# Reordering the softmax, transpose and bookkeeping steps of a causal-attention loop, and the layer-norm and transpose steps of the gating stage, in an eight-core transformer layer

## The chip, the cores and the metric

The kernel runs as one program on the 8 cores of one Trainium2 chip. Each core works on its own share of the rows and no core waits for another. The metric is device time in microseconds (us) of the slowest core. Each core has TensorE (PE: matmuls and transposes, reading SBUF and writing PSUM), VectorE (DVE), ScalarE (ACT), GpSimd (POOL) and SyncE (SP), which run side by side; each works through its own queue in the order of the program, and queues wait for one another on semaphores.

## The reference, cut to what matters

```python
# x: (2, 8192, 1024) float32
def attn(z, qk, ov):                     # one head, width 1024
    scores = einsum('bsd,de,bte->bst', z, qk, z) / 32
    scores = where(causal, scores, -inf)
    return einsum('bst,btd,de->bse', softmax(scores), z, ov)

def ffn(z):                              # 16 experts of width 512, 4 chosen, and a shared one
    scores = softmax(z @ gate_w.T)       # best 2 of 4 groups, then best 4 experts
    y = sum_e c[:, e] * ((silu(z @ w1[e]) * (z @ w3[e])) @ w2[e])
    return y + (silu(z @ ws1) * (z @ ws3)) @ ws2

x = x + attn(layernorm(x)); x = x + ffn(layernorm(x))
```

## The kernel before

Four cores share one of the two sequences. A core owns 16 query tiles (slots m = 0 to 15) of 128 rows, every fourth tile of its sequence; the first stage projects its own rows to Q and the second does the attention, the third the second layer norm with the gating, the fourth the experts. The sums of all slots stay in SBUF in `ACC`.

**Attention.** Keys and values are the normalised rows of the whole sequence. They are made on every core in 8 panels of 1024 rows, each of 8 tiles, into double buffers: V (`VP`) row-wise, K (`KP`) transposed. Panel p is used by slots 2p to 15, so panel 0 has 16 steps, panel 1 has 14, and panel 7 has 2. While panel p is used, panel p+1 is produced in between (`emit_prod_load`, `emit_prod_tp`):

- A load (L394, three buffers `STG`) and a layer norm (`ln_chain`): two passes over the tile on DVE (L254 and L258, sum and sum of squares), three tiny DVE operations (L262 to L268), then on ACT three tiny ones (L271 to L277) and the normalising pass (L281).
- Eight transposes on PE into the single PSUM buffer `PSPT2B` (L403), and one copy into `KP`: on DVE for even tiles (L410), on ACT for odd ones (L414).

A step i of the loop `do_panel`, which treats slot m, puts into the queues, in this order:

- `emit_qk`: 16 matmuls for the scores into `PS_SE` or `PS_SO`, alternating (L437; the first slot has 8, and the first two slots add a mask, L428).
- `emit_softmax`: DVE takes the negated row maximum (L452) and updates the running one (L456, or L460 to L466); ACT takes the exponential of the change (alpha, L469, from panel 1 on), then that of the scores into `PBF` with the row sum (L472); DVE updates the running sum (L478 or L482), which waits for that row sum.
- `emit_t` for step i-1: 8 transposes of `PBF` on PE (L491) into the single PSUM buffer `PSPT` and an ACT copy to `PTS` (L497). The transposes wait for exp(i-1) and for the copy of step i-2.
- `emit_pv` for step i-2: 16 matmuls into the single `PS_PV` (L508), then DVE rescales and adds to `ACC` (L517, or L520).
- Layer norms of the next panel, spread evenly over the steps (two at a time in panels 5 and 6), and transposes of tiles that are four behind.

After the last step come the two outstanding transposes and products, the remaining four production transposes, and `emit_finalize` for two slots: reciprocal (L530), scaling (L534), transposes (L539), the product with `ov` (L556) and the residual (L564, L571).

**Gating.** For each of 16 slots: `do_tt_ln(m)` (layer norm of `ACC` as above, then on DVE a cast to bf16, L716, and the remainder, L719), `do_tt_tp(m)` (PE transposes L726 and ACT copy L732 of the cast; PE transposes L737 and ACT copy L743 of the remainder), and `do_tt_gate(m)` (24 small matmuls L760 on both copies, then the DVE copy L769). The loop is staggered by hand: at m it emits gate(m-2), transposes(m-1), layer norm(m). A chain of small DVE operations then picks the experts, and the experts follow.

Of the kernel before, what the change touches and what calls it, by code (L numbers as in the profile page):

```python
# [166 lines left out]
def build_program(attn_only=False):  # L167
# [21 lines left out]
    with contextlib.ExitStack() as stk:  # L189
# [101 lines left out]
        with (  # L291
# [69 lines left out]
            with (  # L361
# [83 lines left out]
                    P.group("tensor", fns, reads=rd, writes=[rSP], inc="pe")  # L445
                    return nkt, SP, rSP

                def emit_softmax(p, i, m, nkt, SP, rSP):
                    par = i % 2
                    al = i % 3  # L450
                    ext = nkt * 128
                    P.emit("vector", lambda v: v.reduce_max(  # L452
                        smc(C_NRM + par), SP[:, 0:ext], axis=AX.X, negate=True),
                        reads=[rSP], writes=[rNRM[par]], inc="ve")
                    if p == 0:
                        P.emit("vector", lambda v: v.tensor_copy(  # L456
                            smc(C_NM + m), smc(C_NRM + par)),
                            reads=[rNRM[par]], writes=[rNM[m]], inc="ve")
                    else:
                        P.emit("vector", lambda v: v.tensor_sub(  # L460
                            smc(C_TMD + par), smc(C_NRM + par), smc(C_NM + m)),
                            reads=[rNRM[par], rNM[m]], writes=[rTMD[par]])
                        P.emit("vector", lambda v: v.tensor_scalar_min(
                            smc(C_TMD + par), smc(C_TMD + par), 0.0),
                            reads=[rTMD[par]], writes=[rTMD[par]])
                        P.emit("vector", lambda v: v.tensor_add(  # L466
                            smc(C_NM + m), smc(C_NM + m), smc(C_TMD + par)),
                            reads=[rTMD[par], rNM[m]], writes=[rNM[m]], inc="ve")
                        P.emit("scalar", lambda s: s.activation(  # L469
                            smc(C_ALPHA + al), smc(C_TMD + par), AF.Exp),  # L470
                            reads=[rTMD[par]], writes=[rALPHA[al]], inc="sc")
                    P.emit("scalar", lambda s: s.activation(  # L472
                        PBF[:, par * 1024: par * 1024 + ext], SP[:, 0:ext], AF.Exp,
                        bias=smc(C_NM + m), accum_out=smc(C_RSUM + par)),
                        reads=[rSP, rNM[m]], writes=[rPBF[par], rRSUM[par]],
                        inc="sc")
                    if p == 0:
                        P.emit("vector", lambda v: v.tensor_copy(  # L478
                            smc(C_LL + m), smc(C_RSUM + par)),
                            reads=[rRSUM[par]], writes=[rLL[m]], inc="ve")  # L480
                    else:
                        P.emit("vector", lambda v: v.scalar_tensor_tensor(  # L482
                            smc(C_LL + m), smc(C_LL + m), smc(C_ALPHA + al),
                            smc(C_RSUM + par), ALU.mult, ALU.add),
                            reads=[rRSUM[par], rALPHA[al]], writes=[rLL[m]],
                            inc="ve")
# [94 lines left out]
                def do_panel(p):  # L581
                    buf = p % 2
# [4 lines left out]
                    hist = []  # L587
                    for i, m in enumerate(slots):
                        nkt, SP, rSP = emit_qk(p, buf, i, m)
                        emit_softmax(p, i, m, nkt, SP, rSP)  # L590
                        hist.append((p, buf, i, m, nkt))
                        if i >= 1:
                            emit_t(*hist[i - 1])
                        if i >= 2:
                            emit_pv(*hist[i - 2])
                        want_ld = (len(prod) * (i + 1) + n - 1) // n
                        while nld < min(want_ld, len(prod)):
                            emit_prod_load(*prod[nld])
                            nld += 1
                        while ntp < nld - 4:  # L600
                            emit_prod_tp(*prod[ntp])
                            ntp += 1
                    emit_t(*hist[-1])
                    if len(hist) >= 2:
                        emit_pv(*hist[-2])
                    emit_pv(*hist[-1])
                    while nld < len(prod):
                        emit_prod_load(*prod[nld])
                        nld += 1
# [5 lines left out]
                for p in range(NPANEL):  # L615
                    do_panel(p)
# [36 lines left out]
        if True:  # L653
# [43 lines left out]
            if True:  # L697
# [75 lines left out]
                for m in range(NSLOT):  # L773
                    if m >= 2:
                        do_tt_gate(m - 2)
                    if m >= 1:
                        do_tt_tp(m - 1)
                    do_tt_ln(m)
                do_tt_tp(NSLOT - 1)
                do_tt_gate(NSLOT - 2)  # L780
                do_tt_gate(NSLOT - 1)
# [180 lines left out]
def _get_nc(attn_only=False):  # L962
    if attn_only not in _CACHED:
        _CACHED[attn_only] = build_program(attn_only)
    return _CACHED[attn_only]
# [50 lines left out]
```

How the kernel before makes its waits and increments, by code:

```python
        def body(engobj, e):  # L110
            for fn, waits, inc, inc_by in qs[e]:
                for s, v in waits:
                    engobj.wait_ge(self.semh[s], v)
                inst = fn(engobj)
                if inc is not None:
                    inst.then_inc(self.semh[inc], inc_by)
```

## Time and profile before

| | us |
|---|---|
| median of 2 runs | 2742.2 (2741.36 to 2743.04) |
| the profiled execution, time | 2740.59 |
| its span, slowest core (core 6) | 2738.7 |
| spans of the 8 cores | 2729.5 to 2738.7 |
| granted TensorE clock, mean of each core | 0.932 to 0.934 of full speed |
| attention, core 6 | about 206 to 1047 |
| gating, core 6 | about 1047 to 1200 |
| experts, core 6 | about 1200 to the end |

Over the span PE is busy 2287.7 us (84%), DVE 1120.8 (41%) and ACT 638.3 (23%). The page's share of busy time mixes the stages: the experts take more than half of the span with PE nearly always busy, and neither the attention nor the gating looks like them. The time outside the span is 2740.59 - 2738.7 = 1.9 us.

### The profile page before, as it was taken

The page shows a single profiled execution, that of the slowest core. Times are in us where ns is not written, and L with a number is a line of the kernel's source. Part 1 is how long each engine was busy: PE and PEld are TensorE (multiplying, and loading weights), DVE is VectorE, ACT ScalarE, POOL GpSimd, SP SyncE. Part 2 cuts the span into 40 slices and gives each one's busy share as a digit, 9 for nine tenths or more (in the row PEclk, how much of TensorE's full clock was granted, in tenths as well). Part 3 has the DMA queues.
Part 4 walks back from the last instruction along what each step waited for, and adds up shares of the span by engine and source line. Part 5 has one row for each costly group of instructions (what it writes and reads, how often), then busy time and mean ns, then how long its engine had stood idle before and what let it go on. Part 6 is the DMA issues. An engine that isn't in the chain of part 4 may idle for free.

```text
span 2738.7 us, 34373 instructions; the slowest of 8 cores (2729.5 to 2738.7 us)
## 1 busy us (share of the span) xinstructions
PE 2287.7 (84%) x11568; PEld 1058.0 (39%) x11568; DVE 1120.8 (41%) x1647; ACT 638.3 (23%) x949; POOL 32.9 (1%) x66
## 2 busy tenths in 40 slices
PE   1649898978676563359999999999999999999998
PEld 0324444434333232234444444444444444444443
DVE  3335454546456434533323443233432343422433
ACT  3544434434344323520011000110001100011000
POOL 0000000000000000000000000000000000000000
PEclk9969999999998786579999999999999999999999
DMA  6121010201102202022120221202212022120203
GB/s 141 46 80 37 16 62 16 74 35 47 48 31 77 74 19 55 1 47 46 31 47 16 47 47 31 47 16 47 47 31 46 16 47 47 33 45 16 47 0 123
DMA packets 28373, 121.97 MB, mean 45 GB/s; under 512 B 2864, under 2 KB 7216, under 8 KB 21552
## 3 DMA queue, kind: packets, MB, share of 16 engines
q0 software_dynamic: 11936, 60.98, 12.0%
q1 hardware_dynamic: 16272, 58.79, 6.4%
q8 instruction: 103, 1.69, 0.3%
q14 instruction: 62, 0.51, 0.1%
HBM read 172.36 MB, written 8.39 MB: 66 GB/s over the span
## 4 chain that ended last, share of the span: by engine, by line
PE 55%; DVE 1%; issue 0%; DVEq 0%
PE H L886 36%; PE H L912 18%; DVE APR L900 1%; DVE ACC L923 0%; DVEq L113 0%; DVE ACC L929 0%
## 5 line engine op out<-in xcount | busy, mean ns | idle before, releaser
L886 PE MATMUL H<-XF,W1B 128*128 128x512 bf16 x2304 | 522.9, 380 | 14.8 <-PEq L118 14.3
L912 PE MATMUL H<-W2B,APR 128*128 128x512 bf16 x2304 | 505.5, 378 | 29.4 <-DVE APR L900 29.0
L886 PE MATMUL H<-XF,W3B 128*128 128x512 bf16 x2304 | 520.8, 379 | 0.0
L900 DVE TENSOR_TENSOR APR<-SCRF,H 128x1024 bf16<-128x1024 f32 x144 | 175.9, 1221 | 824.5 <-PE H L886 824.5
L896 ACT ACTIVATE SCRF<-H 128x1024 f32<-128x1024 f32 x144 | 147.5, 1024 | 1346.8 <-PE H L886 1346.7
L923 DVE SCALAR_TENSOR_TENSOR ACC<-H,CC,ACC 128x1024 f32<-128x1024 f32 x256 | 328.7, 1284 | 147.4 <-PE H L912 147.0
L886 PEld LDWEIGHTS H<-XF,W1B 128*128 128x128 bf16 x2304 | 224.7, 98 | 290.2 <-issue 23.8
L912 PEld LDWEIGHTS H<-W2B,APR 128*128 128x128 bf16 x2304 | 206.8, 97 | 328.1 <-issue 118.5
L886 PEld LDWEIGHTS H<-XF,W3B 128*128 128x128 bf16 x2304 | 225.4, 98 | 271.8
L508 PE MATMUL PS_PV<-VP,PTS 128*128 128x512 bf16 x1088 | 266.5, 401 | 17.8 <-DVE ACC L520 11.5
L508 PEld LDWEIGHTS PS_PV<-VP,PTS 128*128 128x128 bf16 x1088 | 107.8, 102 | 149.8 <-issue 49.1
L254 DVE TENSOR_SCALAR_CACHE_REDUCE XLNBF<-STG 128x1024 bf16<-128x1024 f32 x80 | 97.3, 1216 | 116.3 <-DMA STG<-x_seq 70.8
L403 PE MATMUL PSPT2B<-IDB,VP 128*128 128x128 bf16 x512 | 47.6, 248 | 105.2 <-ACT SM L274 26.8
L437 PE MATMUL PS_SO<-KP,Q 128*128 128x512 bf16 x576 | 133.8, 386 | 0.0
L437 PE MATMUL PS_SE<-KP,Q 128*128 128x512 bf16 x512 | 120.0, 387 | 0.0
L258 DVE SCALAR_TENSOR_TENSOR XLNBF<-STG 128x1024 bf16<-128x1024 f32 x80 | 98.0, 1226 | 8.6
L520 DVE SCALAR_TENSOR_TENSOR ACC<-ACC,SM,PS_PV 128x1024 f32<-128x1024 f32 x56 | 71.7, 1280 | 68.5 <-PE PS_PV L508 67.1
L491 PE MATMUL PSPT<-IDB,PBF 128*128 128x128 bf16 x544 | 45.7, 230 | 53.9 <-ACT PTS L497 53.7
L322 PE MATMUL PSPT<-IDB,XLNBF 128*128 128x128 bf16 x128 | 16.2, 306 | 85.3 <-ACT XLNT L328 45.7
L271 ACT ACTIVATE SM<-SM,CONST 128x1 f32<-128x1 f32 x96 | 28.2, 294 | 253.4 <-DVE SM L268 253.1
L403 PEld LDWEIGHTS PSPT2B<-IDB,VP 128*128 128x128 bf16 x512 | 38.3, 111 | 119.6 <-issue 113.0
L437 PEld LDWEIGHTS PS_SO<-KP,Q 128*128 128x128 bf16 x576 | 56.8, 100 | 66.9 <-issue 5.8
(117 smaller groups left out, 1297.1 us busy)
## 6 DMA issues: line engine op xcount, KB each, us to landing
STG<-x_seq SPq DMA_DIRECT2D x64, 512.0 KB, 3.6
W1B<-w_img POOLq DMA_DIRECT2D x16, 1024.0 KB, 7.9
W3B<-w_img POOLq DMA_DIRECT2D x16, 1024.0 KB, 9.3
W2B<-w_img POOLq DMA_DIRECT2D x16, 1024.0 KB, 7.8
STG<-x_own SPq DMA_DIRECT2D x16, 512.0 KB, 4.0
XOWNF<-x_own SPq DMA_DIRECT2D x16, 512.0 KB, 4.5
out<-ACC SPq DMA_DIRECT2D x16, 512.0 KB, 2.7
OVB<-ov_img POOLq DMA_DIRECT2D x1, 2048.0 KB, 22.3
```

The source lines that it names most:

```text
L254: P.emit(se, lambda v: v.tensor_scalar(dump, src_ap, 1.0, 0.0, ALU.mult, ALU.add, accum_out=c(LN_MSUM)), reads=[src_res], writes=[rl, rdump])
L258: P.emit(se, lambda v: v.scalar_tensor_tensor(dump, src_ap, 1.0, src_ap, ALU.mult, ALU.mult, accum_out=c(LN_SSQ)), reads=[src_res], writes ...
L403: fns = [(lambda t, dch=dch: t.transpose(PSPT2B[:, dch * 128:(dch + 1) * 128], vslice(buf, kt, dch * 128, 128), IDB[:, :])) for dch in ran ...
L437: sp_=sp_: t.matmul(SP[:, bank * 512:(bank + 1) * 512], qsl(dch, m * 128, 128), kslice(buf, dch, bank * 512, 512), start=st, stop=sp_))
L491: fns = [(lambda t, kt=kt: t.transpose(PSPT2[:, kt * 128:(kt + 1) * 128], PBF[:, par * 1024 + kt * 128: par * 1024 + (kt + 1) * 128], IDB[ ...
L508: fns.append(lambda t, kt=kt, half=half: t.matmul(PS_PV[:, half * 512:(half + 1) * 512], PTS[:, sl3 * 1024 + kt * 128: sl3 * 1024 + (kt + ...
L520: P.emit("vector", lambda v: v.scalar_tensor_tensor(acc(m), acc(m), smc(C_ALPHA + al), PS_PV[:, :], ALU.mult, ALU.add), reads=[rPV, rALPHA ...
L886: wbuf=wbuf, ich=ich, th=th, pi=pi: t.matmul(ps[:, half * 512:(half + 1) * 512], wbuf[:, pi * 4096 + dch * 512 + ich * 128: pi * 4096 + dc ...
L896: P.emit("scalar", lambda s, h1ps=h1ps: s.activation(SCRF32[:, 0:TCH], h1ps[:, 0:TCH], AF.Silu), reads=[rh1], writes=[rSCR[0]], inc="sc")
L900: lambda v, h3ps=h3ps, ich=ich, th=th: v.tensor_mul(APR[:, ich * NT + th * TCH: ich * NT + (th + 1) * TCH], SCRF32[:, 0:TCH], h3ps[:, 0:TCH]),
L912: t.matmul(yp[:, half * 512:(half + 1) * 512], APR[:, ich * NT + tt * 128: ich * NT + (tt + 1) * 128], W2B[:, pi * 4096 + ich * 1024 + hal ...
L923: lambda v, tt=tt, yp=yp, e=e: v.scalar_tensor_tensor(acc(tt), yp[:, :], CC[:, tt * 16 + e: tt * 16 + e + 1], acc(tt), ALU.mult, ALU.add),
```

## The change

It has two parts, and neither adds or drops an operation.

In the attention, `emit_softmax` is split into `emit_max`, `emit_exp` and `emit_llupd`. Step i now emits scores(i), maximum(i), transposes and copy of step i-1, alpha(i) and exp(i), product(i-2), and the update of the running sum of step i-1 (not i). So on ACT the copy of step i-1 stands ahead of exp(i); on DVE the sum's update of step i-1 stands behind the accumulation of step i-2. The last step's update stands behind the last accumulation of the panel. PE's order is unchanged.

In the gating loop the layer norm of slot m is emitted ahead of the transposes of slot m-1. Only ACT has work of both: its three tiny operations and the normalising pass of slot m now stand ahead of the two copies of slot m-1.

```diff
-                def emit_softmax(p, i, m, nkt, SP, rSP):
+                def emit_max(p, i, m, nkt, SP, rSP):
                     par = i % 2
-                    al = i % 3
                     ext = nkt * 128
...
                             reads=[rTMD[par], rNM[m]], writes=[rNM[m]], inc="ve")
+
+                def emit_exp(p, i, m, nkt, SP, rSP):
+                    par = i % 2
+                    al = i % 3
+                    ext = nkt * 128
+                    if p > 0:
                         P.emit("scalar", lambda s: s.activation(
                             smc(C_ALPHA + al), smc(C_TMD + par), AF.Exp),
...
+
+                def emit_llupd(p, i, m):
+                    par = i % 2
+                    al = i % 3
                     if p == 0:
...
                         nkt, SP, rSP = emit_qk(p, buf, i, m)
-                        emit_softmax(p, i, m, nkt, SP, rSP)
-                        hist.append((p, buf, i, m, nkt))
+                        hist.append((p, buf, i, m, nkt, SP, rSP))
+                        emit_max(p, i, m, nkt, SP, rSP)
                         if i >= 1:
-                            emit_t(*hist[i - 1])
+                            emit_t(*hist[i - 1][:5])
+                        emit_exp(p, i, m, nkt, SP, rSP)
                         if i >= 2:
-                            emit_pv(*hist[i - 2])
+                            emit_pv(*hist[i - 2][:5])
+                        if i >= 1:
+                            emit_llupd(p, i - 1, hist[i - 1][3])
...
-                    emit_t(*hist[-1])
+                    emit_t(*hist[-1][:5])
                     if len(hist) >= 2:
-                        emit_pv(*hist[-2])
-                    emit_pv(*hist[-1])
+                        emit_pv(*hist[-2][:5])
+                    emit_pv(*hist[-1][:5])
+                    emit_llupd(p, hist[-1][2], hist[-1][3])
...
                 for m in range(NSLOT):
                     if m >= 2:
                         do_tt_gate(m - 2)
+                    do_tt_ln(m)
                     if m >= 1:
                         do_tt_tp(m - 1)
-                    do_tt_ln(m)
```

## Rows read from the trace of the kernel before

**Rows 1.** Busy us of each engine by stretch: PE, PEld, DVE, ACT, POOL, granted clock.

```profile
206.00:349.00 143.00, 130.36 (x727) 64.33 (x727) 69.77 (x127) 57.01 (x88) 0.00 (x0) 0.95 0.07 24
...
609.00:722.00 113.00, 89.59 (x498) 43.60 (x496) 59.27 (x124) 45.87 (x80) 0.00 (x0) 0.94 0.14 47
...
1047.00:1200.00 153.00, 45.11 (x641) 36.50 (x642) 87.70 (x191) 68.06 (x98) 1.59 (x3) 0.50 0.12 22
...
841.00:873.00 32.00, 19.95 (x95) 9.24 (x94) 19.09 (x42) 13.56 (x25) 0.00 (x0) 0.71 0.21 70
```

**Rows 2.** Who waited for whom, 206 to 1047 us: us in total, times, longest.

```profile
PE PSPT L491 <- ACT PTS L497: 53.7, 22, 6.2
...
DVE SM L482 <- ACT PBF L472: 95.5, 56, 2.8
```

**Rows 3.** Timeline, attention: three products of panel 0, then one step of panel 3.

```profile
255.25 3.62 PE L508 MATMUL PS_PV<-VP,PTS 128*128 128x512 bf16 x16
262.60 3.62 PE L508 MATMUL PS_PV<-VP,PTS 128*128 128x512 bf16 x16
270.40 3.62 PE L508 MATMUL PS_PV<-VP,PTS 128*128 128x512 bf16 x16
...
636.55 1.23 DVE L452 TENSOR_REDUCE SM<-PS_SO 128x1 f32<-128x1024 f32 x1
639.04 1.09 ACT L472 ACTIVATE PBF<-PS_SO,SM 128x1024 bf16<-128x1024 f32 x1
640.41 0.22 DVE L482 SCALAR_TENSOR_TENSOR SM<-SM 128x1 f32<-128x1 f32 x1 [1.84 <-ACT PBF L472]
641.86 1.21 DVE L254 TENSOR_SCALAR_CACHE_REDUCE XLNBF<-STG 128x1024 bf16<-128x1024 f32 x1
645.23 1.23 DVE L452 TENSOR_REDUCE SM<-PS_SE 128x1 f32<-128x1024 f32 x1
```

**Rows 4.** Timeline: first and last maximum of panels 3 to 6, and a late transpose.

```profile
614.25 0.68 DVE L452 TENSOR_REDUCE SM<-PS_SE 128x1 f32<-128x512 f32 x1
...
686.61 1.23 DVE L452 TENSOR_REDUCE SM<-PS_SO 128x1 f32<-128x1024 f32 x1
...
692.24 0.92 PE L491 MATMUL PSPT<-IDB,PBF 128*128 128x128 bf16 x8 [4.85 <-ACT PTS L497]
...
727.14 0.68 DVE L452 TENSOR_REDUCE SM<-PS_SE 128x1 f32<-128x512 f32 x1
...
786.10 1.22 DVE L452 TENSOR_REDUCE SM<-PS_SO 128x1 f32<-128x1024 f32 x1
...
826.16 0.68 DVE L452 TENSOR_REDUCE SM<-PS_SE 128x1 f32<-128x512 f32 x1
...
881.07 1.22 DVE L452 TENSOR_REDUCE SM<-PS_SO 128x1 f32<-128x1024 f32 x1
...
922.74 0.68 DVE L452 TENSOR_REDUCE SM<-PS_SE 128x1 f32<-128x512 f32 x1
...
963.48 1.23 DVE L452 TENSOR_REDUCE SM<-PS_SO 128x1 f32<-128x1024 f32 x1 [7.04 <-PE PS_SO L437]
```

**Rows 5.** Timeline: one slot of the gating, its end, and two ACT copies back to back.

```profile
1100.95 1.21 DVE L254 TENSOR_SCALAR_CACHE_REDUCE XLNBF<-ACC 128x1024 bf16<-128x1024 f32 x1
...
1105.60 1.24 ACT L281 ACTIVATE SCRF<-ACC,SM 128x1024 f32<-128x1024 f32 x1
...
1109.04 1.21 DVE L254 TENSOR_SCALAR_CACHE_REDUCE XLNBF<-ACC 128x1024 bf16<-128x1024 f32 x1
...
1183.51 1.01 ACT L743 COPY XLO<-PT2B 128x1024 bf16<-128x1024 bf16 x1 [0.32 <-PE PT2B L737]
...
1185.73 0.17 DVE L769 COPY LOG<-PG 128x16 f32<-128x16 f32 x1 [1.16 <-PE PG L760]
...
796.80 0.99 ACT L414 COPY KP<-PSPT2B 128x1024 bf16<-128x1024 bf16 x1
797.70 1.01 ACT L497 COPY PTS<-PSPT 128x1024 bf16<-128x1024 bf16 x1
```

## The prediction

> **What bounds the kernel now.** I read the page first, then the busy time by stretch, the waits of each engine, and the timelines of the attention and the gating. By stretch [rows 1], panel 0 of the attention is bound by TensorE: 130.4 us busy of 143. Panel 3 has 89.6 of 113, and in the gating nothing is full: PE 45, DVE 88 and ACT 68 of 153 us, which is what a chain through several engines looks like. The experts are not touched, so all is decided in 206 to 1200 us.
>
> In the attention the largest wait of PE is on ACT's copy to `PTS`, 53.7 us in 22 places, and DVE stands idle 95.5 us before the update of the running sum, in 56 places [rows 2]. They are the same trouble. Where PE is unhindered, products follow one another every 7.35 us, and 7.80 with the eight production transposes in the step [rows 3]. A step of panel 3 took 8.68 us, from maximum to maximum, and DVE was its bound [rows 3]: maximum and tiny operations about 2.10, idle until the row sum of the exponential 1.84 (update at 640.41), update and accumulation 1.45 (640.41 to 641.86), layer norm 3.37 (641.86 to 645.23). Its own work is 2.10 + 1.45 + 3.37 = 6.92 us, less than PE needs; with the wait it is more. Late maxima then give late exponentials and late transposes.
>
> In the gating the period is 8.09 us (1100.95 to 1109.04) [rows 5], through DVE's two passes, ACT's four operations, and DVE's cast and remainder. ACT's two copies lie beside DVE's next passes.
>
> **The change, part by part.**
>
> *The update of the sum, moved behind the next accumulation.* DVE no longer waits for exp(i): update(i-1) reads a sum that has been ready for a step. What stands behind it (the layer norm, and the next maximum) moves up. DVE's step becomes 6.92 us, 7.52 with a KP copy (about 0.6), plus what the accumulation waits for the product. What is late next is that product, and PE at 7.35 or 7.80.
>
> *The copy ahead of the exponential.* In a full step ACT ends a normalising pass 2.48 us after the maximum began: exp(i) started at 639.04, 2.49 after 636.55 [rows 3]. Now copy(i-1) takes 1.0 first and alpha 0.1 to 0.2, so that exp(i) ends some 4.7 us after its maximum began instead of 3.6, or 5.7 where a KP copy on ACT lies before it. Its transposes come a whole PE step after their scores. With DVE about 1 to 2 us behind PE, exp(i) is ready 6 to 7 us after its scores, ahead of the 7.35 or 7.80: hidden in the middle of a panel, not at its two ends. There both the copy and the exponential had to be done before the next transposes in the old order too, since `PSPT` is single; whichever is last, the pair costs the same 2.1 us.
>
> Carried through by hand from maximum to maximum, with PE's own spacings:
> - Panel 3: steps of 4.95, 5.7, 7.1, 7.5, 6.0, 9.35, 7.2, 8.4 and 8.0, together 64.2 us (6.0 and 9.35 are the steps around one without a layer norm, where PE decides). Before: 686.61 - 614.25 = 72.36 [rows 4]. The last transposes, at 692.24 before, start 7.9 us sooner (an exponential now ends the pair).
> - Panel 4 (a layer norm in every step): 4.95, 5.7, 7.1, 7.5, 7.95, 7.2, 8.4, together 48.8, against 786.10 - 727.14 = 58.96 [rows 4]: 10.2 us.
> - Panel 5 (two layer norms in some steps): 8.45, 5.75, 6.9, 17.1, 9.4, together 47.6, against 881.07 - 826.16 = 54.91 [rows 4]: 7.3. The last layer norm, whose ACT part holds up the last copy, gains another exp wait of 1.3: 8.6 us.
> - Panel 6: 8.45, 9.25, 18.1, together 35.8, against 963.48 - 922.74 = 40.74 [rows 4]: 4.9 us. PE waits here for a KP copy behind two layer norms on DVE, so only the waits ahead of them count.
> - Panels 0 to 2, where PE is nearly full, hold 18.3 of the 53.7 us [rows 2]. Of these the first transposes gain 0.95 in each panel, 2.85; small ones in the middle, with what follows them, 3.7; the waits at the ends (9.0) stay but for 1.3. Together 7.8 us.
> - Panel 7 gains 0.5.
> - Against these, the last update of each panel now stands between the last accumulation and the KP copy (or the reciprocal), on the path: 8 x 0.26 = 2.1 us lost.
>
> Sum for the attention: 7.9 + 10.2 + 8.6 + 4.9 + 7.8 + 0.5 - 2.1 = 37.8 us gained. Bounds: if only PE's listed waits on the copy in the middle of panels went, about 25; if PE's clock rises too, 48.
>
> *The gating.* Counted from the end of the normalising pass, 1106.84, DVE's next passes start at 1109.04, after 2.20 us [rows 5]. In the new order ACT's two copies of slot m-1 start only at that end. Back-to-back copies follow each other at 0.90 and the first can begin 0.1 early (796.80 and 797.70) [rows 5], so they are done after 1.80. The gate of m-1 reads the second copy; from the end of that copy to the start of the gate's DVE copy is 1.21 (1183.51 + 1.01 to 1185.73) [rows 5]. The DVE copy of gate(m-1) stands in DVE's queue ahead of the passes of slot m+1, which start some 0.1 after it: 1.80 + 1.21 + 0.1 = 3.11 us instead of 2.20. The period goes from 8.09 to 9.0. Gate copies stand ahead of the passes of slots 2 to 15: 14 x 0.91 = 12.7 us lost. Bounds: 0 if something I missed lets the gate run early; 14 x 1.4 = 19.6 if each ACT operation starts 0.15 to 0.25 after the last instead of overlapping. I take 12.7, since that spacing of copies was measured. At the end of the loop the last copy closes 4.5 us after the last pass in both orders. Everything else in this part is hidden: the transposes of m-1 are done during DVE's passes, as before.
> That an engine's queue is strict in its order is also what the Trainium skill says (PSUM - Partial Sum Buffer, Engine vs sequencer instructions: ScalarE's and VectorE's queues are first in, first out). By that rule the gating must get slower, whatever the attention does; the trace agrees, with no ACT or DVE row here out of program order.
>
> The sum is made against the profiled execution's own 2740.6 us, 1.6 below the median of the runs shown: 2740.6 - 37.8 + 12.7 = 2715.5 us.
>
> **The rivals.**
>
> *The attention gives nothing and the gating decides (slower).* The place is the transposes of step i on PE. exp(i) now ends 1.1 us later after its maximum; if ACT's queue ran so late that the exponential came more than 7.8 us after the scores, every step would wait again, and DVE's freed time would go into waiting for products. It decides when the attention gains less than 12.7 us. With a gain of 0 the time is 2753. For it speaks that ACT's layer-norm part sits in front of copy and exponential in each step; against it, ACT is busy only 45.9 of 113 us in panel 3 [rows 1] and the margin above is 1 to 2 us.
>
> *A smaller gain: early maxima only move the wait to PE's own order.* The accumulation waits for PV(i-2), which runs after the scores and the transposes. If DVE loses what it won there in panels 4 to 6 too, half of their 23.7 us goes: 2727. The steps above have only 0.2 to 0.9 us of such waits, which is why I take the larger gain.
>
> *A larger gain by the clock.* At 841 to 873 us PE's granted clock was 0.71, in a stretch where it was busy 20 of 32 us, and in full panels 0.94 to 0.95 [rows 1]. A product at the low level of 1.2 GHz takes 1.7 us more than at 2.4. If six to eight of them come back to the high level where waits vanish, another 10 to 13 us are won: 2704. Against it: waits of 2 to 4 us remain in each panel, and in panels 5 and 6 those of some 7 us.
> The Trainium skill has this rule (TensorE: Matmul & The Clock Gate, HAM oscillation): pauses of TensorE let it fall back to the lower clock, so that removing pauses pays twice. The clock of 0.71 beside the pauses agrees; the rule would give this rival's 2704, and 2715.5 stands without it.
>
> *The gating's edit costs nothing*, since ACT's copies would end before DVE's remainder: they do (1.80 against 2.20), but the gate's 1.21 comes behind them. If that were wrong, 2703.
>
> **How the numbers follow.** Forecast case, 2706 to 2726: 0.64. Larger gain or free gating, under 2706: 0.14. Smaller gain, 2726 to 2742: 0.14. Attention gives less than the gating takes, above 2742: 0.08. Reaching up to the smaller gain's 2727 and beyond, and down to 2703, the range is 2701 to 2731, which leaves out about 2 in 10. About 2% (55 us) is what a measurement of this kernel can tell from no change: 2686 would need 55 us, more than my upper bound of 48 with the gating free. Faster by over 2%: 0.02; within: 0.97; slower: 0.01.
>
> **What would show it.** DVE's wait on the exponential before the sum's update (95.5 us) falls to near 0, and maxima in panels 3 and 4 come every 7.1 to 8.4 us. PE's wait before L491 falls from 53.7 to below 30, and is then put down to the exponential at 472, not to the copy. The attention ends near 1009 instead of 1047. In the gating a new wait appears: DVE L769 on PE L760, about 0.8 us in each of 14 slots, with a period of 9.0; ACT no longer waits before L732. I am wrong if the attention's stretch shortens by less than 25 us, if the gating's period stays at 8.1, or if PE's waits on `PSPT2B` in panels 5 and 6 grow by what the others lose.

## The result and the profile after

The changed kernel took 2717.7 us (median; lowest 2716.28) against 2741.24 for the kernel before in the same comparisons: a ratio of 0.9916, with a 95% interval of 0.9905 to 0.9927. That is faster, by less than 2%. Most kernels here also have executions in which the cores of a die show a lower granted clock and the time is some per cent longer (three of the ten of the changed kernel, 2944 to 3025 us, with which the median would be 2718.89); times and ratios leave them out throughout. The forecast was 2715.5, range 2701 to 2731. The profiled execution took 2716.28 us, its slowest core (core 7) has a span of 2714.4, the eight cores lie between 2704.6 and 2714.4, and the mean granted clock is 0.933 to 0.935, as before.

The line numbers moved: the maximum is L451, exp L477, the sum's update L491 (L487 in panel 0), the transposes L500, the copy to `PTS` L506, the product L517, the accumulation L529 (L526 in panel 0), the last residual L580. In the gating the cast is L729, the remainder L732, the ACT copies L745 and L756, the gate's matmuls L773 and its DVE copy L782. L254 to L281, L403, L410 and L414 are unchanged.

Busy us by stretch, in the columns of [rows 1]: panel 0, panel 3, panel 5, the gating.

```profile
206.00:347.00 141.00, 128.69 (x719) 63.67 (x718) 67.78 (x127) 57.78 (x88) 0.00 (x0) 0.95 0.07 23
...
597.00:701.00 104.00, 86.86 (x493) 43.09 (x492) 58.02 (x125) 45.71 (x80) 0.00 (x0) 0.93 0.16 52
...
791.00:882.00 91.00, 62.45 (x337) 30.71 (x336) 46.69 (x101) 37.19 (x64) 0.00 (x0) 0.87 0.19 59
...
1009.00:1176.00 167.00, 40.74 (x640) 36.34 (x640) 90.22 (x191) 64.85 (x98) 1.59 (x3) 0.50 0.11 20
```

The work of panel 3 takes 104 us instead of 113; the same work of the gating takes 167 instead of 153. Core 7 of the changed kernel stands beside core 6 of the one before, because each was the slowest of its execution. They are not the same core, and the account of the prediction below also goes by the mean of all eight.

Who waited for whom, 206 to 1020 us (total, times, longest), to be read beside [rows 2]:

```profile
DVE ACC L529 <- PE PS_PV L517: 103.0, 37, 8.2
...
DVE ACC L526 <- PE PS_PV L517: 36.5, 16, 6.9
PE PSPT L500 <- ACT PBF L477: 32.4, 17, 5.0
DVE SM L451 <- PE PS_SE L437: 31.4, 11, 6.8
PE PSPT2B L403 <- ACT SM L274: 28.2, 3, 10.6
...
DVE SM L451 <- PE PS_SO L437: 19.9, 10, 6.0
```

DVE's wait before the sum's update is gone from the list. What DVE waits for now is PE: the products (103.0 + 36.5) and the scores (31.4 + 19.9). In the trace of before these were

```profile
DVE ACC L520 <- PE PS_PV L508: 67.1, 24, 7.7
...
DVE SM L452 <- PE PS_SE L437: 22.9, 9, 7.2
...
DVE SM L452 <- PE PS_SO L437: 10.1, 4, 7.0
DVE ACC L517 <- PE PS_PV L508: 12.5, 8, 3.9
```

so they grew by 78 us while the waits for the exponential (95.5 before the update of panels 1 to 7 and 29.1 before that of panel 0, 124.6 us) vanished. A wait that turns from one for ACT in mid-chain into one for the engine that should be the bound is what success looks like here.

### The profile page after: what moved, and what is told of

It is laid out like the page before. It is cut to its first block, busy times and chain, and to the rows that moved or that the text cites. A ratio compares the mean times of both kernels' runs of the same rounds, so it can differ in the third digit from the quotient of the medians.

```text
span 2714.4 us, 34373 instructions; the slowest of 8 cores (2704.6 to 2714.4 us)
## 1 busy us (share of the span) xinstructions
PE 2276.0 (84%) x11568; PEld 1056.5 (39%) x11568; DVE 1118.3 (41%) x1647; ACT 635.9 (23%) x949; POOL 32.9 (1%) x66
## 4 chain that ended last, share of the span: by engine, by line
PE 55%; DVE 1%; issue 0%; DVEq 0%
PE H L899 37%; PE H L925 18%; DVE APR L913 1%; DVE ACC L936 0%; DVEq L113 0%; DVE ACC L942 0%
## 5 line engine op out<-in xcount | busy, mean ns | idle before, releaser
L899 PE MATMUL H<-XF,W1B 128*128 128x512 bf16 x2304 | 522.5, 380 | 14.8 <-PEq L118 14.3
L517 PE MATMUL PS_PV<-VP,PTS 128*128 128x512 bf16 x1088 | 259.5, 393 | 18.4 <-DVE ACC L529 9.1
L517 PEld LDWEIGHTS PS_PV<-VP,PTS 128*128 128x128 bf16 x1088 | 106.4, 101 | 143.1 <-issue 38.5
L254 DVE TENSOR_SCALAR_CACHE_REDUCE XLNBF<-STG 128x1024 bf16<-128x1024 f32 x80 | 97.3, 1216 | 114.7 <-DMA STG<-x_seq 69.0
L403 PE MATMUL PSPT2B<-IDB,VP 128*128 128x128 bf16 x512 | 49.2, 253 | 93.1 <-ACT SM L274 28.2
L529 DVE SCALAR_TENSOR_TENSOR ACC<-ACC,SM,PS_PV 128x1024 f32<-128x1024 f32 x56 | 71.7, 1280 | 109.8 <-PE PS_PV L517 103.0
L271 ACT ACTIVATE SM<-SM,CONST 128x1 f32<-128x1 f32 x96 | 28.2, 294 | 287.4 <-DVE SM L268 286.9
L773 PE MATMUL PG<-GW,XF 128*128 128x16 bf16 x256 | 11.6, 174 | 94.4 <-ACT XLO L756 93.8
L403 PEld LDWEIGHTS PSPT2B<-IDB,VP 128*128 128x128 bf16 x512 | 39.5, 113 | 107.8 <-issue 101.0
```

The source lines that it names most:

```text
L254: P.emit(se, lambda v: v.tensor_scalar(dump, src_ap, 1.0, 0.0, ALU.mult, ALU.add, accum_out=c(LN_MSUM)), reads=[src_res], writes=[rl, rdump])
L271: P.emit("scalar", lambda s: s.activation(c(LN_VAR), c(LN_VAR), AF.Ln, bias=CONST[:, 2:3]), reads=[rCONST, rl], writes=[rl])
L403: fns = [(lambda t, dch=dch: t.transpose(PSPT2B[:, dch * 128:(dch + 1) * 128], vslice(buf, kt, dch * 128, 128), IDB[:, :])) for dch in ran ...
L517: fns.append(lambda t, kt=kt, half=half: t.matmul(PS_PV[:, half * 512:(half + 1) * 512], PTS[:, sl3 * 1024 + kt * 128: sl3 * 1024 + (kt + ...
L529: P.emit("vector", lambda v: v.scalar_tensor_tensor(acc(m), acc(m), smc(C_ALPHA + al), PS_PV[:, :], ALU.mult, ALU.add), reads=[rPV, rALPHA ...
L899: wbuf=wbuf, ich=ich, th=th, pi=pi: t.matmul(ps[:, half * 512:(half + 1) * 512], wbuf[:, pi * 4096 + dch * 512 + ich * 128: pi * 4096 + dc ...
```

## One step of the attention, one slot of the gating

A step of panel 3 with a layer norm in it, beside the step of [rows 3]:

```profile
621.45 1.23 DVE L451 TENSOR_REDUCE SM<-PS_SO 128x1 f32<-128x1024 f32 x1
...
623.68 1.28 DVE L529 SCALAR_TENSOR_TENSOR ACC<-ACC,SM,PS_PV 128x1024 f32<-128x1024 f32 x1 [0.22 <-DVE SM L465]
623.83 0.99 ACT L506 COPY PTS<-PSPT 128x1024 bf16<-128x1024 bf16 x1
...
624.83 1.10 ACT L477 ACTIVATE PBF<-PS_SO,SM 128x1024 bf16<-128x1024 f32 x1
624.88 0.21 DVE L491 SCALAR_TENSOR_TENSOR SM<-SM 128x1 f32<-128x1 f32 x1
625.01 1.21 DVE L254 TENSOR_SCALAR_CACHE_REDUCE XLNBF<-STG 128x1024 bf16<-128x1024 f32 x1
...
626.71 0.61 PE L500 MATMUL PSPT<-IDB,PBF 128*128 128x128 bf16 x8
...
628.38 1.23 DVE L451 TENSOR_REDUCE SM<-PS_SE 128x1 f32<-128x1024 f32 x1
```

From maximum to maximum are 6.93 us, DVE's own work of 6.92 that the prediction had counted, against 8.68 before. The update at 624.88 starts 0.05 us after exp(i) and waits for nothing, since it reads the sum of step i-1. The exponential ends at 625.93, 4.48 us after its maximum began (forecast: 4.7), and the transposes start at 626.71 with no wait.

A slot of the gating, to be read beside [rows 5]:

```profile
1072.47 1.24 ACT L281 ACTIVATE SCRF<-ACC,SM 128x1024 f32<-128x1024 f32 x1
1073.61 0.99 ACT L745 COPY XF<-PT2A 128x1024 bf16<-128x1024 bf16 x1
...
1074.51 1.01 ACT L756 COPY XLO<-PT2B 128x1024 bf16<-128x1024 bf16 x1
1074.67 1.23 DVE L732 TENSOR_TENSOR XLO<-SCRF,XLNBF 128x1024 bf16<-128x1024 f32 x1
1075.77 0.36 PE L773 MATMUL PG<-GW,XF 128*128 128x16 bf16 x8 [6.68 <-ACT XLO L756]
...
1076.74 0.17 DVE L782 COPY LOG<-PG 128x16 f32<-128x16 f32 x1 [0.83 <-PE PG L773]
1076.99 1.22 DVE L254 TENSOR_SCALAR_CACHE_REDUCE XLNBF<-ACC 128x1024 bf16<-128x1024 f32 x1
```

Both copies now stand behind the normalising pass, the gate's matmuls wait for the second copy, and DVE, which has the gate's copy ahead of its next passes, stands 0.83 us idle. The next slot begins with the pass at 1086.17: a period of 9.18 us.

## The experiments

Two lengths describe each kernel: the attention from its first maximum to the last residual (before 835.5 us, after 799.3), and the gating from there to the first expert matmul (154.3 and 169.3). "Before" in a ratio is the kernel before on the same chip. Times are medians. All are cut from the changed kernel; only the order of emission differs, so where nothing is said all the work is done.

### Each half of the change alone

**att_only** keeps the attention's part and gives the gating its old order.

```diff
-                    do_tt_ln(m)
                     if m >= 1:
                         do_tt_tp(m - 1)
+                    do_tt_ln(m)
```

> The attention's edits alone, the gating loop in its old order. My theory (two independent effects that add): the attention gains 38 us and nothing else changes, 2741.2 - 38 = 2703, with the gating's period back at 8.09 us. Rival (the gating's 15 us loss is partly an effect of the attention ending earlier, for instance through the experts' weight loads): 2710 or more.

Measured: 2704.0 us, ratio 0.9854 (0.9834 to 0.9873); attention 801.7, gating 154.3.

**gate_only** is the reverse: the old attention with the layer norm emitted ahead.

> The gating's edit alone. My theory: the gate's DVE copy, which now waits for ACT's second copy and the 24 small matmuls, holds up the passes of the slot after next, 14 x 1.09 = 15 us: 2756, slower than before, with a period of 9.18 us. Rival (the gating's edit is neutral or helps by itself, and the period of 9.18 comes with the other part): 2741 or less.

Measured: 2755.3 us, ratio 1.0042 (1.0027 to 1.0056); attention 834.8, gating 169.3, period 9.18.

The halves are of opposite sign and add up: 0.9854 + 0.0042 = 0.9896 against 0.9916 measured, within the intervals of the three. The half with the gating is a loss by itself, so the rival in which it costs nothing is refuted.

### Which move in the attention did it

**dve_only** (old gating) leaves ACT's copy in its old place, behind the exponential, and moves only DVE's tiny update.

```diff
                         emit_max(p, i, m, nkt, SP, rSP)
+                        emit_exp(p, i, m, nkt, SP, rSP)
                         if i >= 1:
                             emit_t(*hist[i - 1][:5])
-                        emit_exp(p, i, m, nkt, SP, rSP)
                         if i >= 2:
                             emit_pv(*hist[i - 2][:5])
```

> Old gating; in the attention only the update of the running sum is moved one step later, while ACT keeps the exponential ahead of the copy. My theory (the gain comes from DVE's idle 95 us before that update, the order on ACT matters little): 2701 to 2709, nearly all of the 38 us. Rival (the copy ahead of the exponential carries the gain, since PE's largest wait was on that copy): 2725 or more.

Measured: 2701.8 us, ratio 0.9844 (0.9824 to 0.9863); attention 798.2.

**act_only** (old gating) moves only the copy, and leaves the update ahead of the accumulation, waiting for exp(i).

```diff
                         emit_exp(p, i, m, nkt, SP, rSP)
+                        emit_llupd(p, i, m)
                         if i >= 2:
                             emit_pv(*hist[i - 2][:5])
-                        if i >= 1:
-                            emit_llupd(p, i - 1, hist[i - 1][3])
...
-                    emit_llupd(p, hist[-1][2], hist[-1][3])
```

> Old gating; in the attention only the ACT copy is put ahead of the exponential, while DVE still waits for the row sum of the same step before its accumulation. My theory: DVE now waits about 1.1 us longer in each step where it is the bound (some 25 of 72): slower than before by 15 to 35 us, 2756 to 2776. Rival (copy first carries the gain): 2715 or less.

Measured: 2775.0 us in its profiled execution alone, so with no interval, some 31 more than before on the same chip (2743.8); attention 872.0, which is 36.5 longer. All eight cores show it: their attentions took 863.6 to 872.0 us, against 831.6 to 835.5 before. The waits of its attention, 206 to 1090 us:

```profile
DVE SM L491 <- ACT PBF L477: 124.3, 56, 3.7
...
PE PSPT L500 <- ACT PBF L477: 57.4, 24, 6.2
...
DVE SM L487 <- ACT PBF L477: 36.3, 16, 4.0
PE PS_PV L517 <- DVE ACC L529: 28.8, 24, 1.7
```

DVE waits 124.3 + 36.3 = 160.6 us for the exponential where it waited 124.6, which is 36.0 more: as much as the whole loss. In dve_only these waits are absent, and PE's largest wait of this kind is

```profile
PE PSPT L500 <- ACT PTS L506: 33.1, 18, 5.0
```

This pair is the core of the study. The page of before blamed ACT's copy for 53.7 us of PE's waits. Moving the blamed copy alone costs 36 us; moving a DVE instruction of 0.22 us, whose wait no engine but DVE felt directly, wins the whole 1.5%, and cuts the very wait that names the copy from 53.7 to 33.1. With the update out of the way no worth of the copy's place can be told: 0.9844 and 0.9854 lie inside each other's intervals. The transposes were late because the scores' maxima were late, and those because DVE's queue stood still behind the update.

### The gate emitted later

**gate_late** (changed kernel) was to give the loss back by emitting the gate behind the layer norm and the transposes.

```diff
-                    if m >= 2:
-                        do_tt_gate(m - 2)
                     do_tt_ln(m)
                     if m >= 1:
                         do_tt_tp(m - 1)
+                    if m >= 2:
+                        do_tt_gate(m - 2)
```

> The changed kernel with one move: in the gating loop the gate of slot m-2 is emitted after the layer norm of m and the transposes of m-1, so that its DVE copy stands behind the passes of slot m; ACT keeps the new order, its two copies behind the normalising pass. My theory (the loss comes from the place of the gate's copy in DVE's queue, not from ACT's order itself): the period returns to 8.09 us and the 15 us come back, 2718.9 - 15 = 2704. Rival (ACT's copies behind the pass cost the time by themselves): about 2718.

Measured: 2725.0 us, ratio 0.9939 (0.9922 to 0.9957); gating 174.4, period 9.46. A miss, and the experiment's fault: slots m and m-2 share a buffer, so the remainder of slot m is written into `XLO` before the gate of m-2 reads it. The gate therefore waits for DVE's remainder, and computes with another slot's (this is how the kernel departs from the reference):

```profile
1041.92 0.36 PE L773 MATMUL PG<-GW,XF 128*128 128x16 bf16 x8 [7.03 <-DVE XLO L732]
```

**gate_mid** mends that: the gate of m-2 comes behind the normalising pass of m but ahead of its cast and remainder. (`do_tt_stat` holds DVE's two passes and tiny operations, `do_tt_norm` ACT's part, `do_tt_cast` the cast and the remainder.) ACT's order stays that of the changed kernel.

```diff
-                    if m >= 2:
-                        do_tt_gate(m - 2)
-                    do_tt_ln(m)
+                    do_tt_stat(m)
+                    do_tt_norm(m)
+                    if m >= 2:
+                        do_tt_gate(m - 2)
+                    do_tt_cast(m)
                     if m >= 1:
                         do_tt_tp(m - 1)
```

> The changed kernel, with the gating's order changed once more so that every tile is read before it is written over: DVE passes of slot m, its ACT part, gate(m-2) with its DVE copy, then cast and remainder of m, then the transposes and ACT copies of m-1. ACT keeps the changed kernel's order (copies behind the normalising pass), only the gate's DVE copy has moved, into DVE's idle time. My theory (the loss comes from that copy's place in DVE's queue): the period returns from 9.18 to 8.09 us, 15 us less than the changed kernel, 2704. Rival (ACT's order costs by itself): 2715 or more.

Measured: 2700.7, 2714.9 and 2715.7 us, ratio 0.9875 (0.9833 to 0.9916), with before at 2739 to 2753 in that comparison. The median alone would speak for the rival, but the cores tell the two apart: in the two longer executions cores 2 and 3 had a mean clock of 0.925 to 0.927 and spans of 2709 to 2714, while no other core took more than 2699, which with the 1.9 us outside the span is 2701 (the last section comes back to such pairs of cores). The stage says the same: gating 153.0, period 8.02. ACT's copies still stand behind the normalising pass, and DVE's copy of the gate follows its neighbour with no wait:

```profile
1072.71 0.16 DVE L270 SCALAR_TENSOR_TENSOR SM<-SM 128x1 f32<-128x1 f32 x1
1072.89 0.17 DVE L806 COPY LOG<-PG 128x16 f32<-128x16 f32 x1
```

So late copies are harmless in themselves: only the place of the gate's copy in DVE's queue differs from the changed kernel. The loss is the chain from copy to gate to DVE's queue.

### Overlapping two slots of the gating

**split_gate** and **both_more** tried to put DVE's passes of slot m+1 ahead of the cast of slot m (the second with tp_first's edit, below).

> The kernel with only the sum's update moved (2702 us), and in the gating the DVE statistics of slot m+1 emitted ahead of the cast and remainder of slot m, the gate's copy behind them. My theory (the gating's period is a chain through DVE and ACT, of which 2.6 us per slot are DVE waiting for ACT): the period falls to DVE's own 5.5 us, 15 x 2.6 = 39 us less, 2663. Rival (the transposes that must have read the cast before the statistics of the slot after next write over it, or the PE at its lower clock, take over): a period of 7 us or more, 2685 or more.

> Both of the two last edits together. If they act in different stages they add: about 2652. If one of them lives on the other (for instance by the experts' start or the weight loads), less than their sum by 5 us or more.

Measured: 2703.9 us, 0.9867 (0.9843 to 0.9891), gating 157.6; and 2678.3, 0.9769 (0.9746 to 0.9793). Both missed, and for gate_late's fault in the first place: the cast and remainder of slot m stand ahead of the gate of m-2, so the gate again reads the lane (the buffer that slots of the same parity share) with another slot's remainder in it, and PE's longest wait of the stage is for that:

```profile
PE PG L787 <- DVE XLO L746: 83.7, 14, 6.5
```

There is a second fault: the passes of m+1 write their discarded output into the lane that holds the cast of m-1 before its transposes read it, so these took other data too. Both kernels compute something else than the reference in part of the output, and their times say nothing on the overlap as it was meant.

**split_mid** (dve_only's attention; the lines are against dve_only's gating) puts PE's transposes of the cast (`do_tt_tpa`) ahead of those passes; the two ACT copies and the transposes of the remainder are `do_tt_tpb`. The gate of m-2 stands ahead of cast and remainder of m again.

```diff
+                do_tt_stat(0)
                 for m in range(NSLOT):
-                    if m >= 2:
-                        do_tt_gate(m - 2)
-                    if m >= 1:
-                        do_tt_tp(m - 1)
-                    do_tt_ln(m)
+                    if m >= 1:
+                        do_tt_tpa(m - 1)
+                    if m + 1 < NSLOT:
+                        do_tt_stat(m + 1)
+                    do_tt_norm(m)
+                    if m >= 2:
+                        do_tt_gate(m - 2)
+                    if m >= 1:
+                        do_tt_tpb(m - 1)
+                    do_tt_cast(m)
```

> The kernel with only the sum's update moved (2702 us), and a gating in which the PE transposes of the cast of m-1 come first, then the DVE passes of slot m+1, the ACT part of m, gate(m-2), the ACT copies of m-1, and last cast and remainder of m. Every tile is read before it is written over. My theory (the gating is a chain, and DVE idles 2.7 us a slot for ACT's pass): DVE becomes the bound at 5.5 to 5.9 us a slot, 2661 to 2669. Rival (a chain through ACT's copies remains): 7 us or more a slot, 2685 or more.

Measured: 2674.3 us, ratio 0.9744 (0.9717 to 0.977); gating 115.5, period 5.68. In the gating this is what was foretold, 38.7 us off the stretch; the total lies some 5 us above the expectation's 2669, for a reason told in the last section. In the final kernel (best) a slot of the gating looks so:

```profile
1060.28 0.17 DVE L806 COPY LOG<-PG 128x16 f32<-128x16 f32 x1
...
1060.45 0.69 DVE L746 CAST XLNBF<-SCRF 128x1024 bf16<-128x1024 f32 x1
...
1061.25 1.22 DVE L749 TENSOR_TENSOR XLO<-SCRF,XLNBF 128x1024 bf16<-128x1024 f32 x1
...
1062.60 1.22 DVE L256 TENSOR_SCALAR_CACHE_REDUCE XLNBF<-ACC 128x1024 bf16<-128x1024 f32 x1
...
1065.96 0.17 DVE L806 COPY LOG<-PG 128x16 f32<-128x16 f32 x1
```

None of DVE's instructions waits here, and in the whole loop only three do, by 0.4 to 0.6 us: 5.68 us is DVE's own work for a slot, and a chain through several engines has become a stage bound by one.

### The wait for a KP copy behind two layer norms

The prediction noted that PE waits in panels 5 and 6 for a copy behind two layer norms. The changed kernel still has it: 28.2 us in 3 places in the list above, put down to ACT. In the timeline DVE's copy is what came last before it:

```profile
916.55 0.69 DVE L410 COPY KP<-PSPT2B 128x1024 bf16<-128x1024 bf16 x1
...
917.38 1.01 PE L403 MATMUL PSPT2B<-IDB,VP 128*128 128x128 bf16 x8 [10.64 <-ACT SM L274]
```

**tp_first** is dve_only with the production transposes and their copies emitted ahead of the step's layer norms.

```diff
+                        while ntp < min(want_ld, len(prod)) - 4:
+                            emit_prod_tp(*prod[ntp])
+                            ntp += 1
                         while nld < min(want_ld, len(prod)):
                             emit_prod_load(*prod[nld])
                             nld += 1
-                        while ntp < nld - 4:
-                            emit_prod_tp(*prod[ntp])
-                            ntp += 1
```

> The kernel with only the sum's update moved (2702 us), and in each attention step the production transposes emitted ahead of the layer norms instead of behind them. My theory (PE's remaining waits of 8.8 to 10.6 us in panels 5 and 6 are for a KP copy queued behind two layer norms on DVE; DVE's own work then becomes the bound): these three waits fall below 3 us, and 8 to 15 us are won, 2687 to 2694. Rival (the waits only move to the maxima behind the same layer norms): within 3 us of 2702.

Measured: 2676.8 us, ratio 0.9763 (0.9746 to 0.978), 25 us faster than dve_only, where 8 to 15 were foretold. The wait put down to ACT is gone, and the longest of those that are left is 3.8, not below 3:

```profile
PE PSPT2B L403 <- DVE KP L410: 21.2, 10, 3.8
```

Over eight cores the attention is 26.7 us shorter than in dve_only, and 17.6 of it lie in panels 5 and 6, where the waits were. The other nine lie mostly in panels 1 to 4; what they come from was not looked into, and the granted clock rose as well (panel 6 from 0.76 to 0.82).

**best** is split_mid's gating with tp_first's order.

> The last kernel's gating together with the production transposes ahead of the layer norms in the attention (2677 us by itself against 2742). The stages follow one another, so the gains should add: 2677 - 37 = 2640, within 5 us. If the experts start before their first weights are there, the gain of the gating is cut: 2650 or more.

Measured: 2634.6 us, ratio 0.9598 (0.9572 to 0.9625); gating 115.1. It is 5 us under the 2640 foretold, and the two gains add up: its attention of 770.3 us is tp_first's (773.2), its gating split_mid's (115.5). Four of the six executions of before in this comparison had a pair of cores at a lower clock (last section) and best's had none; against the two without, 2739.2 and 2742.0, the gain is 3.9%.

## Why the prediction was right, point by point

**The chain through DVE (right).** The 1.84 us of waiting in a step are gone and a step takes 6.93 us instead of 8.68; dve_only shows that this move alone carries the gain. The rows behind the 6.92 give 0.08 less: 8.68 - 1.84 is 6.84, because maximum and tiny operations took 2.02 and not 2.10. The prediction's sentence that both waits "are the same trouble" is now shown, not only argued. It had also costed the copy's move at nothing under the cover of a PE step; dve_only against att_only bears that out (2701.8 and 2704.0, not told apart), and act_only shows the price without the cover, 36 us. Of the signs named, the attention ends at 1008.6 (near 1009), and PE's wait before its transposes is put down to the exponential; it fell to 32.4 us, not below 30. The waits on `PSPT2B` that would have refuted it did not grow (28.2 us in 3 places, 26.8 + 9.0 before).

**Panel by panel.** From first to last maximum panel 3 took 63.66 us (forecast 64.2), panel 4 49.24 (48.8), panel 5 48.85 (47.6), panel 6 34.48 (35.8). Panel 3's ends are these, with the last transposes, which now wait for the exponential and not the copy, as foretold:

```profile
603.67 0.69 DVE L451 TENSOR_REDUCE SM<-PS_SE 128x1 f32<-128x512 f32 x1
...
667.33 1.23 DVE L451 TENSOR_REDUCE SM<-PS_SO 128x1 f32<-128x1024 f32 x1
...
672.96 0.61 PE L500 MATMUL PSPT<-IDB,PBF 128*128 128x128 bf16 x8 [2.79 <-ACT PBF L477]
```

They start 69.29 us after the panel's first maximum, 77.99 before: 8.7 us gained, forecast 7.9.

From a panel's first maximum to the next panel's (for panel 7, to the last residual) these are the us gained, for the two slowest cores and as the mean of all eight cores, each against itself:

| panels | forecast | core 6 before, core 7 after | mean of eight cores |
|---|---|---|---|
| 0 to 2 | 7.8 | 8.6 | 10.8 |
| 3 | 7.9 | 8.3 | 8.7 |
| 4 | 10.2 | 8.5 | 10.0 |
| 5 | 8.6 | 6.5 | 5.4 |
| 6 | 4.9 | 4.6 | 4.4 |
| 7 | 0.5 | -0.3 | -0.2 |
| last updates | -2.1 | in the rows above | in the rows above |
| sum | 37.8 | 36.2 | 39.2 |

One core's gain lies between 32.3 and 45.3 us, so a comparison of two different cores can't judge single terms.

**Mis-sized terms.** *Panel 5* was over-rated. Between its maxima it gained 6.3 us (mean; forecast 7.3), and behind the last one it lost 0.8 where a gain of 1.3 was forecast. The hand count let the panel's end move up with the layer norm. But the last copy to `PTS` did not move up as far as the maxima, and the last product waits for it 3.56 us, on all eight cores, where it was 2.4 on seven of them:

```profile
857.66 1.01 ACT L506 COPY PTS<-PSPT 128x1024 bf16<-128x1024 bf16 x1
...
858.92 5.30 PE L517 MATMUL PS_PV<-VP,PTS 128*128 128x512 bf16 x16 [3.56 <-ACT PTS L506]
```

*Panel 4* looks over-rated only on core 6, where the last product had waited 2.39 us before; on the seven others it had waited 4.1, and it waits 4.2 in the changed kernel. *Panels 0 to 2* were under-rated by 3.0, and most of what they gave (6.3 of 10.8) is in panel 2. *The last update of a panel* was costed at 0.26; PE's wait for the KP copy behind it grew from 1.83 to 1.95 or 1.97, so it is 0.13, 1 us in all instead of 2.1. Single panels are not to be read more finely than 3 us: gate_only, with the old attention, has panel 5 at 93.4 us where before has 96.6, and panel 4 at 101.2 where before has 99.0.

**The gating (right in mechanism, short by 2.2 us).** From the end of the normalising pass (1073.71) the second copy ends at 1075.52, after 1.81 (forecast 1.80); the gate's DVE copy starts 1.22 later (forecast 1.21). The term of 0.1 for DVE's next pass was mis-sized: it starts 0.25 after the copy (1076.74 to 1076.99), and the 0.1 was the distance behind a copy that had not waited (last section). So the sum is 3.28 instead of 3.11, and 14 x 0.17 = 2.4 us explains the difference between 12.7 and the measured 169.25 - 154.31 = 14.9. The foretold signs are there: 14 slots in which DVE waits for the gate, a period of 9.18 (9.0), and no wait of ACT before its first copy.

**Why the sum came out close.** On the mean of eight cores the attention gained 39.2 us and the gating lost 14.8: 24.4, where 37.8 - 12.7 = 25.1 was forecast. The attention gave 1.4 more than forecast and the gating took 2.1 more; inside the attention 3.0 more in panels 0 to 2 stand against 3.2 less in panel 5. That such misses cancel is luck. Between the two slowest cores it is 36.2 - 14.9, and another 2.0 us ahead of the attention, whose first maximum stood at 208.03 instead of 210.02. These 2.0 are no effect of the change either: over the eight cores the first maximum lies at 207.2 to 210.1 before and at 207.0 to 210.0 after.

**The rivals.** *The attention gives nothing* needs the exponential more than 7.8 us behind its scores; its mechanism, an exp(i) that ends 1.1 us later, is real, and act_only shows it at work, but only with the update still in its old place. *A smaller gain*: DVE's waits for products did grow by 60 us, but panels 4 to 6 gave 19.9 of the 23.7 us forecast for them (mean), 3.8 short and not 12. *The clock*: a part of this rival came true. Its 1.7 us is not the price of a whole product at the low level: in a product that starts at 769.69 in the changed kernel eight of the 16 matmuls come every 0.42 us and the others every 0.21, and it takes 5.30 us instead of 3.62, so 1.7 is what half a product costs. From first maximum to last residual the two slowest cores show

```profile
210.02:1045.56 835.54, 652.75 (x3559) 319.00 (x3557) 415.31 (x852) 327.89 (x556) 0.00 (x0) 0.91 0.13 44
...
208.03:1007.34 799.31, 646.46 (x3559) 317.67 (x3557) 410.38 (x852) 328.69 (x556) 0.00 (x0) 0.91 0.14 46
```

and on the mean of eight cores PE's busy time for the same matmuls fell from 653 to 643 us, with the granted clock up from 0.901 to 0.911. The other kernels go the same way: gate_only, with the old attention, has 653 us at 0.901, act_only, with more waits, 667 at 0.889, and att_only and dve_only 645 and 643 at 0.906 and 0.910. The mean over the whole span (0.932 to 0.934 before, 0.933 to 0.935 after) hides this, since the experts fill more than half of it and the gating at 0.50 grew longer. By the Trainium skill (TensorE: Matmul & The Clock Gate, HAM oscillation) pauses let TensorE fall back to its lower clock, so removing them should pay a second time; in the attention's clock and busy time the trace agrees. How much of the 39.2 us came this way is not shown; the whole gain was 1.4 above a sum that had no term for it. A single panel can't carry the reading: panel 5 is at 0.81 to 0.84 on all sixteen cores of before and gate_only and at 0.86 to 0.87 on all of the changed kernel, but at 0.81 on four cores of att_only, whose attention is the same.

## What to carry to other kernels

When the profile names an instruction as late, look at what stands still in the queue of the engine that feeds it: a 0.2 us bookkeeping operation that waits in order for another engine can set the pace of a loop, and belongs behind all work that doesn't need its result. When one engine's instruction is moved past another's, follow the moved result to every queue that waits for it in order; ACT's copies were harmless to move until the gate's DVE copy, ahead of the next slot's passes, had to wait for them. A stage with no full engine is a chain: stagger it until one engine never waits, and check of each buffer that it is read before the later slot writes it.

## What the runs showed of the hardware

**A pair of cores at a lower clock.** In split_mid's profiled execution cores 2 and 3 ran panel 1 slowly. Busy time from 362 to 470 us, core 1 and core 2:

```profile
core 1: us, PE busy (x) PEld busy (x) DVE busy (x) ACT busy (x) POOL busy (x), PEclk, DMA share, GB/s
362.00:470.00 108.00, 97.92 (x559) 48.41 (x556) 62.94 (x132) 47.12 (x83) 0.00 (x0) 0.97 0.09 30
...
core 2: us, PE busy (x) PEld busy (x) DVE busy (x) ACT busy (x) POOL busy (x), PEclk, DMA share, GB/s
362.00:470.00 108.00, 106.00 (x500) 49.17 (x508) 58.71 (x124) 46.02 (x83) 0.00 (x0) 0.81 0.09 30
```

Core 2 issued a tenth fewer matmuls in the same time, and its panel 1 took 149.7 us, where core 1 took 132.4. Its span is 2669.7, that of core 3 2669.2, and of the other six 2649.9 to 2656.8. As the metric is the slowest core, this is where the missing 5 us of that expectation went. The other three executions of split_mid are no better (2674 to 2675 us), and each has cores with a mean clock of 0.933 to 0.935 where the rest have 0.940 or more: 2 and 3 again, 0 to 5, and 0 and 1. On the same chip gate_mid has cores 2 and 3 low in two of three executions, and before has one pair (0 and 1, 2 and 3, or 4 and 5) low in four of six; best's three have none, and neither has any execution that counts on the two chips of the other experiments. So the cores fell in pairs, on one chip and in some runs only. What sets it off no run here shows. The Trainium skill (TensorE: Matmul & The Clock Gate, Seeing it yourself) tells of a limiter on current that takes a whole die to 13/16 of the clock when its cores are busy together; 0.81 is that share, but in this execution two cores of a die had it and the six others of the chip, as busy, did not.

**DVE behind an instruction that had waited.** In the kernel before, the gate's copy does not wait and the next pass starts 0.08 us after it; this is the line ahead of the pass at 1100.95 in [rows 5]:

```profile
1100.87 0.17 DVE L769 COPY LOG<-PG 128x16 f32<-128x16 f32 x1
```

In the changed kernel the same copy waits, and the same pass starts 0.25 or 0.26 us after it, in all 14 slots; gate_only and gate_late show the same 0.26. So an instruction behind one that had waited for a semaphore started 0.17 us later. Small as it is, it was the only term of the gating's sum that was wrong by more than 0.01.
